# One attention stage of a sixteen-stage transformer kernel: its loop over the batches written out as a software pipeline, with the layer norm inside and the query and key weights multiplied into one

## What is computed

```python
x = x + _L1_attn_b_ref(_layernorm(x, axis=-1), Wk, Wq, Wv)

def _L1_attn_b_ref(x, Wk, Wq, Wv):
    K = x @ Wk
    Q = x @ Wq
    V = x @ Wv
    scale = 1.0 / math.sqrt(K.shape[-1])
    wei = jnp.einsum('bth,bsh->bts', Q, K) * scale
    ...
    wei = jnp.where(causal, wei, -jnp.inf)
    wei = jax.nn.softmax(wei, axis=-1)
    ...
    return jnp.einsum('bts,bsh->bth', wei, V)
```

## Time and profile before

| | us |
|---|---|
| time, median of 3 runs | 4779.49 (4778.62 to 4785.60) |
| the profiled execution's own time | 4775.26 |
| its span in the trace | 4773.5 |
| TensorE busy | 3025.8 (63%) |
| VectorE busy | 2876.3 (60%) |
| GpSimd busy | 2030.1 (43%) |
| ScalarE busy | 1695.8 (36%) |
| the norm's block, from its first instruction to the end of its last | 24.94 |
| the attention's block, to the end of its last instruction | 116.35 |

### The profile page before, as it was taken

The page is one execution under the profiler, slowest core; times in us unless marked ns, Lnnn a source line. Parts: engine busy times, 40 slices in busy tenths (PEclk is TensorE's granted clock), DMA queues, the critical chain, the costliest instruction groups (busy, mean ns, idle before and its releaser), DMA issues. The chain is left out here.

```text
span 4773.5 us, 68315 instructions
## 1 busy us (share of the span) xinstructions
PE 3025.8 (63%) x23645; PEld 1861.7 (39%) x23645; DVE 2876.3 (60%) x6131; ACT 1695.8 (36%) x2974; POOL 2030.1 (43%) x2621
## 2 busy tenths in 40 slices
PE   5767267765393227577577756577756677666956
PEld 4666111111393126456433324333334333244534
DVE  4624567664345773343367649567568666486768
ACT  2422255553131113242335532255511355313511
POOL 6543311000344003303344449244486354386676
PEclk9788578886596658787789967599967799776867
DMA  5122222210131001101122200222100322000000
GB/s 148 39 81 67 67 73 60 61 38 1 62 95 39 0 35 55 35 0 54 46 78 75 55 1 0 54 62 75 29 1 0 82 62 74 2 0 1 1 0 18
DMA packets 218170, 206.27 MB, mean 43 GB/s; under 512 B 50439, under 2 KB 195015, under 8 KB 217080
## 3 DMA queue, kind: packets, MB, share of 16 engines
q1 hardware_dynamic: 205560, 176.85, 13.5%
q0 software_dynamic: 12288, 25.19, 1.8%
HBM read 103.55 MB, written 96.47 MB: 42 GB/s over the span
## 5 line engine op out<-in xcount | busy, mean ns | idle before, releaser
L918 DVE TENSOR_REDUCE l0b_negm<-l0b_ps_s 128x2 f32<-128x1024 f32 x256 | 302.7, 1219 | 166.6 <-PE l0b_ps_s L698 166.3
L786 ACT ACTIVATE l0b_E<-l0b_ps_t 128x1024 f32<-128x1024 f32 x256 | 261.8, 1023 | 231.0 <-PE l0b_ps_t L680 230.8
L918 DVE TENSOR_REDUCE l3a_negm<-l3a_ps_s 128x2 f32<-128x256 f32 (+3 forms) x256 | 199.0, 817 | 92.9 <-PE l3a_ps_s L704 92.7
L918 DVE TENSOR_REDUCE l2b_negm<-l2b_ps_s 128x2 f32<-128x256 f32 (+3 forms) x256 | 199.1, 818 | 89.9 <-PE l2b_ps_s L704 89.2
L918 DVE TENSOR_REDUCE l2a_negm<-l2a_ps_s 128x2 f32<-128x256 f32 (+3 forms) x256 | 198.9, 818 | 88.2 <-PE l2a_ps_s L704 88.1
L786 ACT ACTIVATE l3a_E<-l3a_ps_t 128x768 f32<-128x768 f32 (+1 forms) x192 | 169.1, 881 | 186.9 <-PE l3a_ps_t L680 186.6
L786 ACT ACTIVATE l2a_E<-l2a_ps_t 128x768 f32<-128x768 f32 (+1 forms) x192 | 169.2, 881 | 180.6 <-PE l2a_ps_t L680 180.4
L786 ACT ACTIVATE l2b_E<-l2b_ps_t 128x768 f32<-128x768 f32 (+1 forms) x192 | 169.2, 881 | 153.9 <-PE l2b_ps_t L680 153.8
L862 POOL TENSOR_SCALAR_AFFINE_SELECT l2b_E<-l2b_E 128x256 f32<-128x256 f32 x256 | 100.9, 408 | 221.1 <-ACT l2b_E L786 221.1
L862 POOL TENSOR_SCALAR_AFFINE_SELECT l3a_E<-l3a_E 128x256 f32<-128x256 f32 x256 | 101.0, 406 | 220.6 <-ACT l3a_E L786 218.4
L862 POOL TENSOR_SCALAR_AFFINE_SELECT l2a_E<-l2a_E 128x256 f32<-128x256 f32 x256 | 101.0, 406 | 215.0 <-ACT l2a_E L786 212.4
(11 more groups left out here) (997 smaller groups left out, 9516.6 us busy)
## 6 DMA issues: line engine op xcount, KB each, us to landing
l0b_stack<-l0b_q_piece SPq DMA_DIRECT2D x48, 128.0 KB
l0b_stack<-l0b_k_piece SPq DMA_DIRECT2D x48, 128.0 KB
room_up<-l0b_stack SPq DMA_DIRECT2D x32, 192.0 KB, 3.5
room_down<-l0b_stack SPq DMA_DIRECT2D x32, 192.0 KB, 4.4
l2a_stack<-l2a_q_piece SPq DMA_DIRECT2D x48, 128.0 KB
l2a_stack<-l2a_k_piece SPq DMA_DIRECT2D x48, 128.0 KB
room_up<-l2a_stack SPq DMA_DIRECT2D x32, 192.0 KB, 4.0
room_down<-l2a_stack SPq DMA_DIRECT2D x32, 192.0 KB, 4.9
```

The lines of the kernel that those rows point to most:

```text
L786: act.activation(probs(n % 3, c, 0)[:, 2 * p:2 * p + 2, :], ps_t[:, :, 0:width[c]], ACT.Exp, scale=scale).then_inc(probs_ready.sem, 1)
L918: e = dve.tensor_reduce(negm[:, qt, :, j], ps_s[n % 2][:, :, off:off + keys[qt]], AX.X, ALU.max, negate=True)
```

## The change

The separate norm block of this stage is gone (`layer1_attention_b` no longer calls `norm_stage`); RowNorm's pieces stand in the attention's streams. The loop is unrolled: step (i, qt) for i from -2 to 9 and qt from 0 to 3 makes the scores and exponentials of batch i, transposes the probabilities of batch i - 1 and multiplies them by the values one step later, projects batch i + 1, normalises batch i + 2, and makes the statistics of batch i + 3. The buffers that live across this are doubled or tripled. The queries' and keys' projections become one: at the stage's start TensorE multiplies the two weight matrices (`wqk`, scaled by 1/sqrt(128)), and the scores are (x Wq Wk^T) x^T, with the normalised input itself in the place of the keys. So L1185, L1219 and L1214's copy have no counterpart, and the scaling of the maximum (L1244) is gone with the scale. The values' copy moves from VectorE to ScalarE, the addition to X from VectorE to GpSimd. `lay_out` gives the query and key weights transposed. RowNorm works with any number of banks, and has one here.

```diff
     def transposes(self, pe, b):
         pe.wait_ge(self.norm_ready.sem, self.norm_ready.upto(b + 1))
-        if b >= 2:
-            pe.wait_ge(self.T_ready.sem, self.T_ready.upto(b - 1))
+        if b >= len(self.banks):
+            pe.wait_ge(self.T_ready.sem, self.T_ready.upto(b - len(self.banks) + 1))
...
+            def scores(b, qt):
+                m, n = b * TB + qt, P * (qt + 1)
+                if qt == 0:
+                    pe.wait_ge(qT_ready.sem, qT_ready.upto(b + 2))
+                if m >= 2:
+                    pe.wait_ge(probs_ready.sem, probs_ready.upto(m - 1))
+                pe.matmul(ps_s[m % 2][:, 0:n], qT[b % 2][:, qt * P:n], core.XNT[:, b * S:b * S + n], start=True, stop=False,
+                          skip_group_check=True)
...
+            pe.matmul(ps_q[:, 0:D], w[:, 0:D], w[:, D:2 * D], start=True, stop=True).then_inc(qT_in_psum.sem, 1)
+            for i, qt in steps():
+                if 0 <= i < B:
+                    scores(i, qt)
+                if 0 <= i + 1 < B and qt == 1:
+                    queries(i + 1)
+                if 0 <= i + 1 < B and qt == 2:
+                    values(i + 1)
+                if 0 <= i + 2 < B and qt == 2:
+                    rows.transposes(pe, i + 2)
+                if 0 <= i - 1 < B:
+                    probs_back(i - 1, qt)
+                m = (i - 1) * TB + qt - 1
+                if 0 <= m < B * TB:
+                    attend(m // TB, m % TB)
...
+            for i, qt in steps():
+                if 0 <= i < B:
+                    exponentials(i, qt)
+                if 0 <= i + 2 < B and qt == 1:
+                    rows.normalise(act, i + 2)
...
+        @block.gpsimd
+        def _(pool):
+            for i in range(-2, B + 2):
+                if 0 <= i + 2 < B:
+                    rows.roots(pool, i + 2)
+                if 0 <= i - 2 < B:
+                    b = i - 2
+                    pool.wait_ge(out_read.sem, out_read.upto(b + 1))
+                    x = core.X[:, b * TB:(b + 1) * TB, :]
+                    pool.tensor_tensor(x, x, y[b % 2][:, :, :], ALU.add).then_inc(out_added.sem, 1)
...
+            rows.statistics(dve, ch, 0)
+            for i, qt in steps():
+                if 0 <= i < B:
+                    maximum(i, qt)
+                if 0 <= i + 2 < B and qt == 0:
+                    rows.shifts(dve, i + 2)
+                if 0 <= i - 1 < B:
+                    read_probs(i - 1, qt)
+                if 0 <= i - 2 < B and qt == 0:
+                    divide(i - 2)
+                if 0 <= i + 3 < B and qt == 3:
+                    rows.statistics(dve, ch, i + 3)
...
 def layer1_attention_b(core):
-    norm_stage(core, "l1b_norm")
     single_head_attention_stage(core, "l1b", core.w["l1b_w"])
```

More of the change, by code:

```diff
@@ L1150, in psum @@
             return ctx.enter_context(nc.psum_tensor(f"{name}_{n}", shape, dt))
[L1152 to L1163, removed]
+        wqk = sb("wqk", [P, D])
@@ L1165, in single_head_attention_stage @@
         ps_e = [psum(f"ps_e{n}", [P, S]) for n in range(2)]
[L1166 to L1169, removed]
-        block = ctx.enter_context(nc.Block())
[L1172 to L1178, removed]
+        rows = RowNorm(core, sb, [ps_n[:, :]])
@@ L1180, in _ @@
         @block.tensor
         def _(pe):
[L1182 to L1185, removed]
-                for t in range(TB):
[L1187 to L1207, removed]
@@ new lines, in queries, with values @@
+            def queries(b):
+                rows.wait_T(pe, b)
+                pe.wait_ge(qT_ready.sem, qT_ready.upto(b + 1))
+                pe.matmul(ps_q[:, :], wqk[:, :], core.XNT[:, b * S:(b + 1) * S], start=True, stop=True).then_inc(qT_in_psum.sem, 1)
+            def values(b):
+                if b >= 1:
+                    pe.wait_ge(v_ready.sem, v_ready.upto(b))
+                for t in range(TB):
+                    mm = pe.matmul(ps_v[:, t * D:(t + 1) * D], core.XNT[:, b * S + t * P:b * S + (t + 1) * P], w[:, 2 * D:3 * D],
+                                   start=True, stop=True)
+                mm.then_inc(v_in_psum.sem, 1)
@@ new lines, in probs_back, with attend @@
+            def probs_back(b, qt):
+                m = b * TB + qt
+                pe.wait_ge(probs_ready.sem, probs_ready.upto(m + 1))
+                if m >= 2:
+                    pe.wait_ge(probsT_ready.sem, probsT_ready.upto(m - 1))
+                for kt in range(qt + 1):
+                    tr = pe.transpose(ps_e[m % 2][:, kt * P:(kt + 1) * P], E[b % 2][:, qt, kt * P:(kt + 1) * P], core.identf[:, :])
+                tr.then_inc(probsT_in_psum.sem, 1)
+            def attend(b, qt):
+                pe.wait_ge(probsT_ready.sem, probsT_ready.upto(b * TB + qt + 1))
+                if qt == 0:
+                    pe.wait_ge(v_ready.sem, v_ready.upto(b + 1))
+                    if b >= 1:
+                        pe.wait_ge(out_read.sem, out_read.upto(b))
+                for kt in range(qt + 1):
+                    mm = pe.matmul(ps_o[:, qt * D:(qt + 1) * D], ET[b % 2][:, qt, kt * P:(kt + 1) * P], v[b % 3][:, kt, :],
+                                   start=(kt == 0), stop=(kt == qt), skip_group_check=True)
+                if qt == TB - 1:
+                    mm.then_inc(out_ready.sem, 1)
@@ L1261, in linear_attention_stage @@
+            dve_step.per = ch.k
+    core.end(1, sig)
+    rows.end()
 def linear_attention_stage(core, name, w, masks, v_scale):
@@ L3096, in lay_out @@
     put("l1a_bo", row(a["L1_attn_a_bout"]))
-    put("l1b_w", np.concatenate([a[f"L1_attn_b_W{n}"] for n in "qkv"], 1))
+    put("l1b_w", np.concatenate([a["L1_attn_b_Wq"].T, a["L1_attn_b_Wk"].T, a["L1_attn_b_Wv"]], 1))
     put("l1f_gate", a["L1_ffn_Wg"])
```

103 lines of the change are left out of this document (63 added, 40 removed).

## The result

The changed kernel took 4732.45 us (median of 4 runs, 4727.56 to 4741.45), the kernel before on the same chip 4782.15 (4 runs, 4778.62 to 4785.6): a ratio of 0.9899, 95% interval 0.9882 to 0.9915, or 49.7 us less. The forecast was 4734.7. Both were measured once more later, on one chip, with 6 and 11 runs: 4744.73 against 4796.4, ratio 0.990 (0.9878 to 0.9921).

What follows compares the result with a forecast made beforehand. The prediction took a chain through one batch as the bound, then a three-engine cycle of 11.0 us a batch. Its terms summed to 97.1 us against 141.88, 44.8 less, giving 4734.7 us; 8-in-10 range 4724 to 4749.

Steps and rivals of the forecast that it cites:

- What bounds the stage: Norm and loop, 141.88 us before: no engine fills the loop, which is a chain through one batch.
- The ring: Dependency cycle through VectorE, GpSimd's power, ScalarE and TensorE, setting the period of batches 2 to 5: 11.0 us a batch.
- ScalarE's piece: In the cycle setting the period: exponential of 256 columns with readout, and normalisation of batch b+3, 2.2 us.
- VectorE's piece: In the cycle setting the period: maxima, copies, statistics, wait for GpSimd's power, shift, reciprocal and division, 6.1 us.
- TensorE's waits: In the middle batches: longest at the norm's transposes (L425) and the scores (L1198), TensorE some 75% busy.
- Fill and batch 0: Stage start: 11.5 us to the first scores, then 7.5 us for batch 0, midway between upper and lower clock.
- Batches 6 and 7, drain: Stage end: nothing left to normalise, so 8.0 and 6.5 us; then drain 9.5 and exit 0.6 us.
- The product of the weights alone would be a small edit: Merged query-key weights: drops the keys' projection, 0.86 us of TensorE a batch, 6.9 us in eight.
- Rival 1: Middle batches: handoffs overlap better and TensorE is the bound, 9.0 us a batch, program 4726; 13%.
- Rivals 2 and 4: Clock low through batches 0, 1 and part of 2, 4742, 12%; or low all stage, 4782 to 4790, 2%.
- Rival 3: Middle batches take 12.5 us through costlier TensorE waits, or the exit takes longer: 4741 to 4746; 18%.
- The prediction fails if another stage changes by more than 2 us: Failure test on stages outside the edited norm and attention: none should change by more than 2 us.

Runs made afterwards that it cites:

- doubled power: Changed kernel with GpSimd's power of every batch computed a second time ahead of the one used; stage 96.1 us against 89.0.
- doubled projection: Changed kernel with the merged query-key projection issued twice into the same bank; stage 91.7 us against 89.0.
- early statistics: Changed kernel with VectorE's statistics of batch i+3 made after query block 1, not 3; stage 81.3 us against 89.0, program 4740.56 us, ratio 0.9883.
- merged loop: Kernel before, norm ahead and hardware loop kept, with only the merged query-key weights; stage 119.1 us against 141.9 or 137.2, program ratio 0.996.
- all of the merge put back: Changed kernel with projection issued twice, its ScalarE copy made twice and each maximum scaled by 1.0 separately; stage 93.7 us against 89.0.

## Why the prediction was right, point by point

- **What bounds the stage: right.** A chain through one batch in which no engine is full. But I took the period of before as "some 14" without asking why one turn took 12.53 and the next 13.87. What the earlier trace rows calls a full turn is a window of 14 us, longer than the turn of 12.53 in it. The granted clock, 0.88 over the loop and 1.00 over that window, would have told that a part of the loop's time was the clock's.
- **The ring: right in its order, too long by 1.1 us.** The doubled power, the doubled projection and the early statistics each moved the time as the ring says. ScalarE's piece was varied in no run and rests on the timeline alone. Mis-sized were VectorE's piece (5.3, forecast 6.1: its instructions don't stand 0.05 us apart but overlap by 0.08, as the copy that starts 0.61 behind a maximum of 0.69, and from the end of the statistics to the shift it was 1.12, forecast 1.29) and the handoffs (0.15, forecast 0.5). Four batches: 4.1 us; batch 1 was too long by another 1.0.
- **TensorE's waits: half wrong.** I expected the longest at L425 and L1198, and TensorE busy for 75%. In batches 2 to 5 the longest, 1.00 to 1.37 us, is at L1219 for the division, which the ring of the prediction leaves out; at L425 it is 0.26, and TensorE is busy for 8.62 of 9.88 us.
- **Fill and batch 0: 2 us too long.** The first scores came 10.8 us after the first statistics (forecast 11.5), and the clock rose near 2001.7, 1.7 us after them, so that less of batch 0 ran at 1.2 GHz than the middle that I took.
- **Batches 6 and 7, drain: right**, 14.06 for 14.5 and 9.52 for 10.1. GpSimd's last addition, 1.26 us, is in the drain as its row had it.
- **"The product of the weights alone would be a small edit": wrong.** I priced TensorE's work (0.86 us a batch) on an engine that wasn't full, and left out the copy and the scalings, which stand in the chain, and the clock. The merged loop saved 18.2 or 22.8 us. In the pipeline the same price, 6.9 in all, was too high: the doubled projection cost 2.6, and all of the merge put back 4.7.
- **Rival 1, TensorE as the bound at 9 a batch: didn't happen** in this kernel, but it is what the early statistics make true, at 8.20.
- **Rivals 2 and 4, the clock low for longer or throughout: didn't happen.** It was 1.00 from 2002 to the stage's end. The Trainium skill, in "TensorE: Matmul & The Clock Gate", Part 4: PE-mode transpose, says that full clock doesn't engage for the transpose mode. Here fourteen transposes stand among the 58 TensorE instructions of a batch's window, and it ran at 1.00, so at that share they didn't keep the clock down.
- **Rival 3, a longer ring: didn't happen.** The ring was shorter than forecast. The rival's own range was off too: 6 us and up to 3 on top of 4734.7 end at 4744, not 4746.
- **"The prediction fails if another stage changes by more than 2 us":** this test was badly chosen. Stages that nothing touched moved by more than that between two executions of one program. The near hit of the program's time, 2.3 us, is luck: the sum behind it missed the stage's length by 8.1 us. Of these, 3.2 are missing in the program's saving (49.7 against the stage's 52.85), and 2.7 are hidden because the median of before was 4782.15 in the result and 4779.49 in the forecast's base.

## What to carry to other kernels

An instruction's price is where it stands: in batches 2 to 5 of the pipeline, 0.86 us a batch more of TensorE's work beside the ring cost nothing, and some 0.3 us a batch of scaling inside it, with a doubled copy on ScalarE, cost 1.2 in the four, so trace the ring through the in-order streams before counting busy time. When work is taken into a pipeline, start what has the longest reply (here statistics and GpSimd's power) a step or two ahead of its reader: changing one number in the code was worth as much (7.7 us) as bringing in the whole norm (7.6). Edits that remove the same waiting don't add up, so run each alone, and both. And look at the granted clock turn by turn before a loop's length is taken as the base of a sum.

## What the runs showed of the hardware

- In a loop with TensorE busy for 9.29 of 12.53 us the granted clock fell to 0.50 for about 3.4 us in two turns after the first in one execution and in five in another (the stage 137.2 and 141.9 us). With the same 9.29 us in turns of 11.67 it stayed at 1.00 for 70 us, in one execution. In the pipeline with the doubled power it fell once, in one batch of four, behind a wait of 2.35 us.
- Fourteen transposes in a batch of 8.20 us, all of it busy, left the clock at 1.00.
- A duplicated float32 projection of 512 columns cost 0.82 to 0.87 us a batch at the upper clock where TensorE was in the path, and nothing where it stood waiting anyway.
- Untouched work of the same program took 2646.5 us in one execution and 2667.6 in another, with 0.781 and 0.777 as the granted clock of the whole span.
